# A transformer block on one core: the last softmax group's reciprocal in two halves, one peak scan moved forward, and the feed-forward part's x roundings placed ahead of its peak scans

## What is computed

```python
x = x + cross_attention(layernorm(x), ctx, ctx, Wq, bq, Wk, bk, Wv, bv, Wo, bo)   # x: (16, 256, 512), 16 heads of 32, rope, causal
def ffn(x):                                   # x = layernorm(x), 4096 tokens of 512
    x = act_qdq(x)                            # scale = max|x| / 32767, round, clip, times scale
    up = act_qdq(x @ lpbq_dequant(w_up).T)    # 4-bit weights in blocks of 32, inner size 1536
    gate = act_qdq(x @ lpbq_dequant(w_gate).T)
    sig = fixed_qdq_u16(sigmoid(gate))
    gate = act_qdq(gate * sig)
    return act_qdq(gate * up) @ lpbq_dequant(w_down).T
x = x + ffn(layernorm(x))
```

## Time and profile before

| what | value |
|---|---|
| median of 3 runs | 1499.49 us (1498.81, 1499.49, 1502.97) |
| the profiled execution's own time | 1501.97 us |
| its span, first to last instruction | 1500.1 us |
| PE busy | 1370.2 us, 91% |
| DVE busy | 1180.3 us, 79% |
| ACT busy | 967.2 us, 64% |
| POOL busy | 343.3 us, 23% |
| mean granted clock of TensorE | 0.969 of full speed |

### The profile page before, as it was taken

How to read it: one execution, slowest core, us unless ns; L and a number is a source line. 1 busy time by engine, 2 the same in 40 slices (tenths; PEclk the granted TensorE clock), 3 DMA queues, 4 the chain that set the end, 5 groups by cost and what they waited for, 6 DMA issues and landing times.

```text
span 1500.1 us, 24408 instructions
## 1 busy us (share of the span) xinstructions
PE 1370.2 (91%) x9186; PEld 771.5 (51%) x9186; DVE 1180.3 (79%) x1790; ACT 967.2 (64%) x2025; POOL 343.3 (23%) x326
## 2 busy tenths in 40 slices
PE   4899999999999999969999999999999308999999
PEld 4566676666666666634444444444444103444444
DVE  6878888888888888756888987888898899565541
ACT  6988888888888887765322224898887894222210
POOL 0544455544445554430111110000000000000000
PEclk9999999999999999989999999999999758999999
DMA  6111111111111111133533333676788999567732
GB/s 230 47 58 58 64 71 71 58 64 71 72 72 58 58 43 43 36 121 125 176 110 123 129 117 134 242 249 240 249 307 298 376 395 354 183 232 236 238 100 84
DMA packets 101556, 224.74 MB, mean 150 GB/s; under 512 B 8768, under 2 KB 21184, under 8 KB 99776
## 3 DMA queue, kind: packets, MB, share of 16 engines
q1 hardware_dynamic: 100864, 219.00, 41.1%
q10 hardware_dynamic: 576, 4.19, 0.9%
HBM read 140.32 MB, written 82.84 MB: 149 GB/s over the span
## 4 chain that ended last, share of the span: by engine, by line
PE 41%; DVE 6%; issue 5%; ACT 2%; DMA 1%; SPq 0%; POOL 0%; ACTq 0%; POOLq 0%; DVEq 0%
PE ffn_banks L1271 24%; PE ffn_banks L1286 17%; DVE qg L1584 3%; DVE ffn_peaks L1470 1%; ACT qg L1385 1%; DMA ffn_ring<-gates_dram 1%; DVE ffn_rest L1578 1%; DMA ffn_rest<-w_parts_dram 0%; ACT ffn_rest L1333 0%; DVE ffn_wide L1463 0%; ACT qg L1360 0%; ACT ffn_ring L1389 0%; DVE ffn_ring L1560 0%; DVE ffn_rises L1468 0%; ACT ffn_ring L1398 0%
## 5 line engine op out<-in xcount | busy, mean ns | idle before, releaser
L1271 PE MATMUL ffn_banks<-ffn_wide,ffn_rest 128*128 128x512 f16 x2304 | 502.1, 381 | 6.1 <-DVE ffn_wide L1458 2.7
L1271 PEld LDWEIGHTS ffn_banks<-ffn_wide,ffn_rest 128*128 128x128 f16 x2304 | 226.1, 98 | 281.8 <-DMA ffn_rest<-w_parts_dram 5.8
L1286 PE MATMUL ffn_banks<-ffn_rest,ffn_wide 128*128 128x512 f16 x1152 | 251.7, 382 | 70.4 <-DVE ffn_wide L1614 70.4
L1286 PEld LDWEIGHTS ffn_banks<-ffn_rest,ffn_wide 128*128 128x128 f16 x1152 | 113.4, 98 | 208.7 <-issue 74.7
L640 ACT ACTIVATE qg<-score_banks,neg_max 128x128 f32<-128x128 f32 (+1 forms) x512 | 208.2, 450 | 18.8 <-DVE neg_max L512 18.8
L1423 ACT ACTIVATE ffn_u_steps<-ffn_ring,ffn_scales 128x1024 int16<-128x1024 f32 x48 | 55.0, 1148 | 156.9 <-DMA ffn_ring<-ups_dram 136.3
L417 POOL TENSOR_TENSOR qg<-qg,per_sum 128x512 f32<-128x512 f32 x64 | 85.9, 1342 | 267.1 <-DVE per_sum L516 267.1
L1333 ACT ACTIVATE ffn_rest<-ffn_banks,ffn_row_back 128x1024 f32<-128x1024 f32 x66 | 73.0, 1106 | 99.3 <-PE ffn_banks L1271 95.7
L419 POOL TENSOR_TENSOR qg<-qg,per_sum 128x1024 f32<-128x1024 f32 x64 | 133.7, 2088 | 0.0
L640 ACT ACTIVATION_READ_ACCUMULATOR qg<-score_banks,neg_max 128x1 f32 x512 | 121.1, 237 | 0.0
L649 ACT ACTIVATE pt<-ring_banks 128x512 f32<-128x512 f32 x128 | 70.3, 610 | 41.7 <-PE ring_banks L776 40.8
(11 more groups left out here) (191 smaller groups left out, 2688.3 us busy)
## 6 DMA issues: line engine op xcount, KB each, us to landing
ffn_ring<-ups_dram SPq DMA_DIRECT2D x44, 512.0 KB, 5.9
ups_dram<-ffn_rest SPq DMA_DIRECT2D x42, 512.0 KB, 3.3
ffn_wide<-ups_dram SPq DMA_DIRECT2D x13, 1024.0 KB, 13.7
gates_dram<-ffn_rest SPq DMA_DIRECT2D x24, 512.0 KB, 2.6
ffn_ring<-gates_dram SPq DMA_DIRECT2D x24, 512.0 KB, 4.6
signs_dram<-qg SPq DMA_DIRECT2D x24, 512.0 KB, 4.1
qg<-signs_dram SPq DMA_DIRECT2D x48, 256.0 KB, 6.5
ffn_rest<-w_parts_dram SPq DMA_DIRECT2D x36, 256.0 KB, 4.1
```

The costliest lines, as they stand in the source:

```text
L1271: last = pe.matmul(banks[:, pair_of(s), half, :], w[:, m % 2, wp, c, :], xq[:, xp, n, c, :], start=(k == 0), stop=(k == 3 * DC - 1))
L1286: last = pe.matmul(down_banks[:, g % 2, t, :], oq[:, g % 2, op, m, t * P:(t + 1) * P], w_down[:, wp, wk, c], start=(start and k == 0), sto ...
```

## The change

It has three parts.

1. For s = 63 the reciprocal is two instructions. The first covers heads 0 and 1, waits until their row sums are there (`last_exped`) and signals a new semaphore, for which POOL's norm waits; the second covers heads 2 and 3 and waits for all row sums, as before.
2. The `peak` of batch 14 stands right behind `dnorm` in DVE's plan instead of behind `otlo` of group 3; `whole_plan` drops the second occurrence.
3. In the feed-forward part ACT rounds blocks 0 to 3 ahead of everything, then two blocks ahead of each of the first two evacuations. DVE splits all eight blocks ahead of its first peak scan.

An unused semaphore (`a_scaled`) is dropped.

```diff
@@ whole_plan
         for step in steps_of_line(line, i):
-            plan.append(step)
+            if step not in plan:
+                plan.append(step)
             plan += after.get((i, step[0], step[1]), [])
@@
-DVE_AFTER[BATCH - 1, "recip", 3] = [("dnorm", 3, BATCH - 1)]
+DVE_AFTER[BATCH - 1, "recip", 3] = [("dnorm", 3, BATCH - 1), ("peak", 0, BATCH - 2)]
@@ POOL, norm
-                    pool.wait_ge(sums_ready, s + 1)
+                    if s == BATCH * GROUPS - 1:
+                        pool.wait_ge(half_sums_ready, 1)
+                    else:
+                        pool.wait_ge(sums_ready, s + 1)
@@ DVE, recip
+                    if s == BATCH * GROUPS - 1:
+                        dve.wait_ge(last_exped, HG // 2)
+                        dve.reciprocal(per_sum[:, s % 2, :, 0:HG // 2], row_sum[:, s % 2, :, 0:HG // 2]).then_inc(half_sums_ready, 1)
+                        dve.wait_ge(exped, s + 1)
+                        dve.reciprocal(per_sum[:, s % 2, :, HG // 2:HG],
+                                       row_sum[:, s % 2, :, HG // 2:HG]).then_inc(sums_ready, 1)
+                        continue
@@ feed_forward, ACT
-            round_x(0)
-            round_x(1)
+            for n in range(4):
+                round_x(n)
             for s in range(NP):
-                if s + 1 < PIECES:
-                    round_x(2 * s + 2)
-                    round_x(2 * s + 3)
+                if s + 2 < PIECES:
+                    round_x(2 * s + 4)
+                    round_x(2 * s + 5)
                 evacuate(s)
@@ feed_forward, DVE
-            split_x(0)
-            split_x(1)
+            for n in range(NG):
+                split_x(n)
             for s in range(NP):
-                if s + 1 < PIECES:
-                    split_x(2 * s + 2)
-                    split_x(2 * s + 3)
                 peak_of(s)
```

More of the change, by code:

```diff
@@ L281, in attend @@
         normed, half_normed, last_filled, last_exped = sem("normed"), sem("half_normed"), sem("last_filled"), sem("last_exped")
+        half_sums_ready = sem("half_sums_ready")
         w_in, w_rounded, w_hi = sem("w_in"), sem("w_rounded"), sem("w_hi")
@@ L960, in feed_forward @@
         u_backed = sem("u_backed")
-        g_scaled, a_scaled, u_scaled = sem("g_scaled"), sem("a_scaled"), sem("u_scaled")
+        g_scaled, u_scaled = sem("g_scaled"), sem("u_scaled")
         gate_in = [sem(f"gate_in{b}") for b in range(2)]
```

## The result

| | before | changed |
|---|---|---|
| median of 13 runs each | 1498.7 us | 1502.61 us |
| lowest to highest | 1493.91 to 1502.97 | 1500.41 to 1508.37 |
| ratio, 95% interval | | 1.0031 [1.0019, 1.0043] |
| profiled execution (span) | 1501.97 (1500.1) | 1502.61 (1500.7) |

The changed kernel is slower by 0.31%, 4.6 us by the ratio and 3.9 us by the medians. The ratio compares runs taken in alternation, so it is the better measure of the two. In the changed kernel's file the lines lie 2 to 12 further on: L405 is L407, L417 and L419 are L422 and L424, L516 is L522 and L524 (the two halves), L520 and L522 are L532 and L534, L527 is L539, L549 is L561, L665 is L677, L776 is L788, L806 is L818, L1271 is L1283, L1333 is L1345. In the kernels of the experiments the lines are shifted by a few again; the tile names tell which instruction a row is.

What follows compares the result with a forecast made beforehand. PE's unbroken 1,584 gate and up matmuls (342.04 us) bound the kernel, so delays ahead of them count. 3.5 (`Oc`) + 2.0 (clock) - 1.3 (feed-forward) = +4.2 us on the median of 1499.49: 1503.7 us, range 1499.6 to 1506.2.

Steps and rivals of the forecast that it cites:

- The delay of `Oc`: End of attention: PE's `Oc` starts at 656.3 instead of 652.67, 3.6 us later; 3.5 taken into the sum.
- The collision: POOL's bias addition L405 meets DVE's `dnorm`; both read SBUF and exclude each other, so `half_normed` comes at 652.1, not 650.35.
- The peak's wait: DVE's moved peak waits for ACT's normalisation of batch 14's second tile, to 654.6, holding `otlo` and `Oc` behind it.
- the two orders that the text left open: DVE's first `dnorm` product or POOL's L405 goes first; either way the second product ends at 652.1 to 652.15.
- The clock: PE's clock falls to half in the stops before `Oc`, costing 2.0 us; bounds 0 and 3.3.
- The feed-forward part: Start of feed-forward: roundings and splits first remove PE's waits up to the fourth evacuation, gaining 1.3 us; bounds 0.7 and 1.4.
- a term that the text had set at nothing on average: Low-clock stretch ahead of the feed-forward part, in both kernels; length may differ by a microsecond either way.
- the sign that the text named: Feed-forward part: 15.6 us between the matmuls of the first and fourth evacuation would show the gain.
- L405 and `dnorm` do not meet: Rival at the end of attention: `Oc` 1.4 us late, about +0.1 without a clock fall, 1499.6 us; 13%.
- The clock stays full: Rival: PE's clock does not fall between the transposes and `Oc`; +2.2, 1501.7 us; 17%.
- The peak's wait is off the path: Rival: the wait delays nothing or DVE's old order holds; first and third parts gain 1.3 each, 1496.9 us; 3%.
- The low clock lasts through the whole projection: Slower rival: half clock through the rest of the projection, `O` included, +3.3 instead of 2.0; +6.2 in all, 1505.7 us; 17%.

Runs made afterwards that it cites:

- e3: Changed kernel with the peak back behind `otlo` and POOL's last bias addition waiting until `dnorm` is through; 1494.13 us, ratio 0.9973 against the kernel before.
- e2: Changed kernel with POOL's last bias addition waiting until `dnorm` is through; 1499.88 us, ratio 1.0009 against the kernel before.
- e1: Changed kernel with the peak of batch 14 back at its old place behind `otlo`; 1496.66 us, ratio 0.9998 against the kernel before.
- e4: Changed kernel with unused 512-column matmuls in PE's two stops, ten ahead of `PT`'s second part, twelve ahead of `Oc`; 1500.01 us, ratio 1.0014 against before.
- e5: Kernel before with the feed-forward edit only; 1497.28 us, ratio 0.9996 against the kernel before.
- e7: Kernel before with only the peak of batch 14 moved, reciprocal whole, old feed-forward part; 1504.32 us, ratio 1.0039 against the kernel before.
- e6: Kernel before with both attention edits, halved reciprocal and moved peak, old feed-forward part; 1507.33 us in 6 runs, ratio 1.0065 against the kernel before.
- e11: The changed kernel profiled once more, without any edit; 1503.73 us, span 1501.8.
- e9: Kernel before with the halved reciprocal only, old peak and old feed-forward part; 1500.16 us, ratio 1.0 against the kernel before.
- e10: The kernel before profiled once more, without any edit; 1496.81 us, span 1495.0.

## Why the prediction was right

It forecast 1503.7 us and no measurable change or a little slower; the median is 1502.61, and the ratio 1.0031 lies at the bound of 0.3% that it gave. With 13 runs each the interval, 1.0019 to 1.0043, leaves out no change, so the measurement told more than that bound said.

**The delay of `Oc`, forecast +3.6 us, measured 7.74 - 4.00 = +3.74.** The runs take it apart, and the parts add up. The halved reciprocal, with nothing beside `dnorm`, gives 4.00 - 2.30 = 1.70 (e3). The collision costs 2.20 with the peak in front (changed less e2) and 4.49 - 2.30 = 2.19 without it (e1 less e3). The peak's wait costs 7.74 - 4.49 = 3.25 with the collision (changed less e1) and 5.54 - 2.30 = 3.24 without it (e2 less e3). -1.70 + 2.20 + 3.25 is 3.75. The rows of before had shown each piece: two instructions that take turns, and `pte` of s = 63 ahead of the normalisation. Put on the clock of the first profile, by adding 1.22, POOL's first product starts at 647.31 (forecast 647.35) and takes 0.61 (0.6), POOL is through at 648.92 (648.95), `dnorm` ends at 652.12 (652.1), and `Oc` starts at 656.41 (656.3). Of the two orders that the text left open it was POOL's bias addition that went first. The text then took 3.5, since 0.1 was to come back at `x2` with the peak no longer in front of it. Next to nothing came back: from `Oc` to `x2` at full clock it is 4.76 us with the peak moved (e4) and 4.78 with it in its old place (e1, e3).

**The clock, forecast +2.0, measured 2.2.** From `Oc` to `x2` the changed kernel takes 6.93 us; before it was 4.79, and with PE kept busy 4.76 (e4). The argument, two long stops where one of 2.19 had done nothing, came out in both profiles of the changed kernel. It was less certain than it looked from one trace: e5 and e7 show that the stop of 2.19 us itself lets the clock fall in some executions. The Trainium skill (TensorE: Matmul & The Clock Gate, HAM oscillation) describes a kernel whose clock is throttled again in the waits for DMA between its groups of matmuls, 3 to 5 us each. The prediction took from it that this term is sure, which is more than the page says: no stop ahead of `PT` or `Oc` here is longer than 3.09 us. What the traces show is this. In all five executions with a stop of 3.03 to 3.09 us ahead of `Oc` and no fillers (changed, e2, e6, e7, e11) the clock fell in it or inside `Oc`; with the stop of 2.62 or 2.63 us alone it stayed full (e1, e9), and with the one of 2.18 or 2.19 us it stayed full in two executions (before, e10) and fell in two (e5, e7).

**The feed-forward part, forecast -1.3.** With the low stretch taken out, that is half of the time from the first gate matmul to the rise of the clock, 4.95 us before and 6.0 after, the fourth evacuation comes at 24.67 - 2.48 = 22.2 before and at 23.87 - 3.0 = 20.9 after. That is 1.3. A pair of values without this working says the same. In e2, e3 and e7 the clock was back about 3 us after the first gate matmul, and PE then stopped 0.54 to 0.70 us inside its first piece, until block 1 was split. The row of e2:

```profile
679.34 20.89 PE L1285 MATMUL ffn_banks<-ffn_wide,ffn_rest 128*128 128x512 f16 x96 [0.70 <-DVE ffn_wide L1477]
```

So an early rise brings no more, and where the clock was back within 4.5 us the fourth evacuation stands at 23.18 to 23.19 us with the edit (e2, e3, e5) and at 24.49 to 24.50 without it (e7, e9), 1.31 apart. Between e6 and the changed kernel, both with 6.0 us of low clock, it is 25.15 - 23.87 = 1.28. Against before only 0.8 of it shows. This is a term that the text had set at nothing on average, and that was wrong by 0.5 us: all three executions with both attention edits and no other change to attention (changed, e6, e11) have 5.9 to 6.0 us of low clock behind the first gate matmul, the two of the kernel before 4.8 and 4.95. In all five the clock was low for 13.65 us on end; but in the three it fell only 7.6 to 7.7 us ahead of the first gate matmul, and before 8.7 and 8.9. So more of the low stretch lies over the matmuls. With the edit, the low stretch ended 2.8 (e2), 4.5 (e5), 5.4 (e1) and 6.0 us (changed) after the first gate matmul, and the fourth evacuation stood at 23.18, 23.18, 23.56 and 23.87: what lies behind 4.5 us costs about half its length. Why it fell later there was not tried. The first evacuation came 10.75 instead of 7.81 us after the first gate matmul, 2.94 later (forecast about 3), and cost nothing, as said. For the same reason the sign that the text named, 15.6 us from the first to the fourth evacuation, could not be seen (it was 13.12); the 5.18 us from the third to the fourth show what it was meant to show.

**The sum.** From the reciprocal to the fourth evacuation the change costs 5.88 + 0.22 - 0.80 = +5.3 us in the first pair and by the same steps 5.4 in the second (e11 less e10); the forecast was +4.2, the ratio says 4.6 with an interval of 2.8 to 6.4. The forecast lacked 0.1 on `Oc`, nearly 0.2 on the clock, 0.1 that the peak did not give back, 0.2 ahead of the first gate matmul and 0.5 in the feed-forward part. In both pairs the kernel before has the clock full at `PT`; in e5, where it fell there, `x2` came 1.67 us later. If that happens in half of the executions of before, as in two of four here, the average difference is some 0.8 us smaller, about 4.5. That is an estimate from four executions. The absolute forecast added its 4.2 us to 1499.49, the median of three runs; over 13 runs of before it is 1498.7, and the forecast would have been 1502.9. The late stop of 2.40 us and the clock's fall behind it, 3.7 us that e10 does not have, did not enter the sum, since the difference and not the changed kernel's span was forecast. They show how far one profiled execution can lie from another. The text used this stop as a row on the clock and did not ask how often it is there.

**The rivals.** "L405 and `dnorm` do not meet" is what e2 makes: `Oc` 1.54 late (forecast 1.4), ratio 1.0009, 1.4 us slower than before (forecast 0.1). The second half of it was wrong: it reckoned with a full clock, and the clock fell all the same, which cost 1.6 us from `Oc` to `x2`. "The clock stays full" is e4, ratio 1.0014, 2.1 us (forecast 2.2). "The peak's wait is off the path" forecast 2.6 us faster than before. With the peak back, e1 has a ratio of 0.9998, whose interval ends at 0.9985, 2.2 us: no change. The halved reciprocal gave no 1.3 there; with the collision it lost 0.5. Only with the collision gone too (e3) is the kernel that much faster. "The low clock lasts through the whole projection" had its point of decision wrong: the clock had not risen when `Oc`'s six matmuls were through, and yet `O`, at 661.16, ran at full clock, since it waits for copies anyway, and the clock was back 1.5 us ahead of it. The price was 2.2, not 3.3.

## What to carry to other kernels

Before a step is moved ahead in an engine's in-order queue, look at what it waits for and at what is queued behind it: here a scan with 2.6 us to wait stood in front of the copy that PE's next matmuls needed, and took 3.25 us. An engine that is released sooner also starts its next instruction sooner; ask which one that is and beside what it will run. One wait that put the bias addition back behind the products turned an edit that gained nothing (e9) into one that gained 1.7 us, and the kernel with it and the feed-forward edit (e3) is 0.27% faster than before. And take more than one profile of each kernel before differences of a few microseconds are read from a pair of spans.

## What the runs showed of the hardware

- When a DVE and a POOL product with two inputs each in SBUF began at the same time (both at 647.66), POOL's ran in its usual 2.35 us and DVE's was recorded with 2.63 instead of 0.42. The wait is inside the recorded duration and not in the idle time ahead of it. All six profiles with this pair show it, 2.63 to 2.64 (changed, e1, e4, e6, e9, e11). With POOL held back it is 0.42 again (e2, e3).
- POOL's product of 256 elements takes 0.61 us alone (at 646.09, changed) and 0.85 beside DVE's.
- One and the same stop of PE, 2.18 to 2.19 us ahead of `PT`, left the clock full in two executions of the kernel before and let it fall in e5 and e7, where the instructions ahead of it are the same. With it the eight transposes take 1.09 us or 1.70 to 1.97.
- The clock can fall after PE has resumed: in e2 the first matmuls of `Oc` still ran at 0.38 us and the last two at 0.63.
- The wait for the load of `w_parts` late in the up stage was between nothing and 2.40 us in the profiles of these kernels. At 2.40 (before) the clock fell, and 144 matmuls took 32.94 us; at 1.85 (changed) and 1.80 (e9) it did not, and they took 31.25.
